# Attention scores of two heads at a time: each head contracted by its own 64 rows of the array, into its own bank, two pairs of heads to a group

## The reference, cut to what matters

```
q, k = rotary_xpos(l2norm(q) * qs, l2norm(k) * ksc)      # 8 heads of 64 channels
sim  = einsum('bhwid,bhwjd->bhwij', q * 8, look_around(k))  # 128 queries x 256 keys
attn = softmax(where(mask, -max, sim))
out  = einsum('bhwij,bhwjd->bhwid', attn, look_around(v))
x    = x + out @ wo
```

## Time and profile before

| | us |
|---|---|
| median of 3 executions | 1212.52 |
| lowest, highest | 1208.71, 1213.76 |
| span of the profiled execution | 1215.7 |
| PE busy in it | 1095.3 |
| DVE, ACT, POOL busy in it | 760.1, 545.0, 364.5 |
| score matmuls (L1719) busy in it | 118.0 |

### The profile page before, as it was taken

The page is one execution under the profiler, slowest core; times in us unless marked ns, Lnnn a source line. Parts: engine busy times, 40 slices in busy tenths (PEclk is TensorE's granted clock), DMA queues, the critical chain, the costliest instruction groups (busy, mean ns, idle before and its releaser), DMA issues.

```text
span 1215.7 us, 18344 instructions
## 1 busy us (share of the span) xinstructions
PE 1095.3 (90%) x5768; PEld 891.3 (73%) x5768; DVE 760.1 (63%) x1886; ACT 545.0 (45%) x1188; POOL 364.5 (30%) x364
## 2 busy tenths in 40 slices
PE   5899799999998898999987699989999898889987
PEld 3677667767686787878876477778878787768776
DVE  7778873666558676667665244666667666644463
ACT  4667423030313565555555233435565555543332
POOL 5212421122124553444440000154435444300020
PEclk9899899999999899999999799999999999999989
DMA  8001020000000000000001000000000000000011
GB/s 303 1 1 52 18 91 1 1 0 0 1 1 19 1 2 18 0 18 0 18 10 53 26 9 9 4 15 2 1 18 0 18 0 26 3 9 9 9 35 35
DMA packets 14330, 25.35 MB, mean 21 GB/s; under 512 B 848, under 2 KB 11208, under 8 KB 13512
## 3 DMA queue, kind: packets, MB, share of 16 engines
q1 hardware_dynamic: 14280, 24.72, 6.2%
HBM read 20.53 MB, written 2.10 MB: 19 GB/s over the span
## 4 chain that ended last, share of the span: by engine, by line
PE 62%; DVE 16%; issue 7%; ACT 6%; DMA 6%; POOL 2%; DVEq 0%; SPq 0%; POOLq 0%; ACTq 0%
PE bank L1433 21%; PE bank L1746 7%; PE bank L1719 7%; DMA shifted<-inner 5%; PE bank L1764 5%; PE bank L1625 5%; PE bank L1577 4%; PE bank L1731 4%; PE bank L1845 3%; DVE conv L585 2%; ACT probs_t L1322 2%; ACT probs L1311 1%; PE bank L1588 1%; DVE scores L897 1%; PE bank L1757 1%
## 5 line engine op out<-in xcount | busy, mean ns | idle before, releaser
L1311 ACT ACTIVATE probs<-scores,row_bias,q_rnorm 128x256 f32<-128x256 f32 (+1 forms) x256 | 144.5, 566 | 161.8 <-DVE row_bias L902 160.8
L1746 PEld LDWEIGHTS bank<-v_tok,probs_t 128*128 128x128 f32 x896 | 114.7, 193 | 50.5 <-ACT probs_t L1322 28.0
L1746 PE MATMUL bank<-v_tok,probs_t 128*128 128x64 f32 x896 | 120.9, 275 | 33.5 <-ACT probs_t L1322 18.6
L1719 PE MATMUL bank<-k_t,q_heads 128*128 128x256 f32 (+1 forms) x512 | 118.0, 364 | 8.4 <-DVE q_heads L886 6.8
L897 DVE CUSTOM_DVE_ANT_0 scores<-bank,mask 128x256 f32<-128x256 f32 (+1 forms) x256 | 89.3, 385 | 26.5 <-PE bank L1719 23.1
L1719 PEld LDWEIGHTS bank<-k_t,q_heads 128*128 128x128 f32 x512 | 87.0, 194 | 17.7 <-issue 8.0
L470 POOL TENSOR_TENSOR norms<-norms,minus_half 128x16 f32<-128x16 f32 x32 | 93.6, 2924 | 2.7
L1433 PE MATMUL bank<-wqkv_hi,x_hi 128*128 128x512 f32 x192 | 89.6, 467 | 1.4 <-ACT v_tok L1288 0.8
L1433 PE MATMUL bank<-t_hi,wm_hi 128*128 128x512 f32 (+1 forms) x192 | 78.2, 407 | 14.1 <-DVE hidden L1055 12.5
L1433 PE MATMUL bank<-wqkv_lo,x_hi 128*128 128x512 f32 x192 | 78.8, 410 | 0.0
L1731 PE MATMUL bank<-ident,probs 128*128 128x128 f32 x448 | 72.8, 280 | 6.2 <-ACT probs L1311 6.2
(11 more groups left out here) (220 smaller groups left out, 2698.2 us busy)
## 6 DMA issues: line engine op xcount, KB each, us to landing
w_stage<-in_wm_l_dram SPq DMA_DIRECT2D x8, 534.0 KB, 3.6
w_stage<-in_wqkv_dram SPq DMA_DIRECT2D x2, 1536.0 KB, 8.0
out_dram<-stream SPq DMA_DIRECT2D x4, 512.0 KB, 2.9
shifted<-inner SPq DMA_DIRECT2D x8, 254.0 KB
stream<-in_x_dram SPq DMA_DIRECT2D x1, 1536.0 KB, 13.2
emb<-in_ctx_dram SPq DMA_DIRECT2D x1, 1536.0 KB, 6.6
inner<-in_w_gate_dram SPq DMA_DIRECT2D x1, 1152.0 KB, 9.3
ew<-in_pos_bias_dram SPq DMA_DIRECT2D x1, 1024.0 KB, 9.8
```

The lines of the kernel that those rows point to most:

```text
L1311: act.activation(probs[:, i % 2, e, 0:nk], scores[:, i % 2, e, 0:nk], ACT.Exp, bias=row_bias[:, w % 2, h:h + 1], scale=q_rnorm[:, w, h:h + 1],
L1719: ins = pe.matmul(bank[6 + i % 2][:, e * 2 * P:e * 2 * P + nk], q_heads[:, 2 * i + e, :], k_t[:, i, k0:(w + 1) * P], start=True, stop=True)
L1746: ins = pe.matmul(bank[3][:, h * DH:(h + 1) * DH], probs_t[:, i % 2, 2 * e + k, :], v_tok[:, w - nk + 1 + k, h * DH:(h + 1) * DH], start=( ...
```

## The change

`q_t` holds the four transposed blocks of q as they are, two heads to a block, without zeros. ACT copies all of it (`queries`); `q_odd` of DVE and the zeroing by POOL are gone. The scores of two pairs are made together: `score_pairs(n, w, 0)` for pairs 0 and 1 stands where `score` 0 and 1 stood, and `score_pairs(n, w, 1)` for pairs 2 and 3 where `score` 2 stood; nothing is left where `score` 3 stood. Each product contracts 64 rows, 0 to 63 for the even head and 64 to 127 for the odd one; even heads go to bank 6 and odd ones to bank 7. `c_qk` counts groups, so `masked` of either pair waits for the whole group, and a group waits until all four masks of the group before it are done.

```diff
-            def q_odd(n):
-                dve.wait_ge(c_t, 2 * n + 2)
-                dve.tensor_copy(q_heads[64:128, :, :]...[:, 1, :, :], bank[2][64:128, :]...).then_inc(c_qo, 1)
...
             def masked(n, w, i, first=False):
-                wait_alone(dve, c_qk, u + 1)
+                wait_alone(dve, c_qk, 2 * n + i // 2 + 1)
                 for e in range(2):
-                    ... bank[6 + i % 2][:, e * 2 * P:e * 2 * P + nk],
+                    ... bank[6 + e][:, (i % 2) * 2 * P:(i % 2) * 2 * P + nk],
...
-            def q_even(n):
+            def queries(n):
                 act.wait_ge(c_t, 2 * n + 2)
-                act.activation(q_heads[0:64, :, :]...[:, 0, :, :], bank[2][0:64, :]..., ACT.Copy).then_inc(c_qe, 1)
+                act.activation(q_t[:, :, :], bank[2][:, :].rearrange("p (c t) -> p c t", t=P), ACT.Copy)\
+                    .then_inc(c_qt, 1)
...
-            def score(n, w, i):
-                u = 4 * n + i
-                if i == 0:
-                    pe.wait_ge(c_qe, n + 1)
-                    pe.wait_ge(c_qo, n + 1)
-                if not (isinstance(u, int) and u < 2):
-                    pe.wait_ge(c_tt, 2 * u - 2)
+            def score_pairs(n, w, g):
+                if g == 0:
+                    pe.wait_ge(c_qt, n + 1)
+                if not (isinstance(n, int) and n == 0 and g == 0):
+                    pe.wait_ge(c_tt, 8 * n + 4 * g)
                 k0 = max(w - 1, 0) * P
-                for e in range(2):
-                    nk = (w + 1) * P - k0
-                    ins = pe.matmul(bank[6 + i % 2][:, e * 2 * P:e * 2 * P + nk], q_heads[:, 2 * i + e, :],
-                                    k_t[:, i, k0:(w + 1) * P], start=True, stop=True)
+                nk = (w + 1) * P - k0
+                for i in (2 * g, 2 * g + 1):
+                    for e in range(2):
+                        half = slice(e * DH, (e + 1) * DH)
+                        ins = pe.matmul(bank[6 + e][:, (i % 2) * 2 * P:(i % 2) * 2 * P + nk], q_t[half, i, :],
+                                        k_t[half, i, k0:(w + 1) * P], start=True, stop=True)
                 ins.then_inc(c_qk, 1)
...
                     transpose_probs(n, w, 0)
-                    score(n, w, 2)
+                    score_pairs(n, w, 1)
...
                         project_o(n - 1)
                         free = [(c_res, n)]
-                    score(n, w, 3)
                     weigh_values(n, w, 1)
...
                     if one:
-                        score(n + 1, (w + 1) % TT, 0)
-                        score(n + 1, (w + 1) % TT, 1)
+                        score_pairs(n + 1, (w + 1) % TT, 0)
                     transpose_o(n, free)
```

More of the change, by code:

```diff
@@ L169, in build @@
         rope_l = sb("rope_l", [P, 4, TT, DH])
-        q_heads = sb("q_heads", [P, HEADS, P])
+        q_t = sb("q_t", [P, KI, P])
         squares = sb("squares", [P, 2, INNER])
@@ L220, in build @@
         (c_zero, c_tab, c_xs, c_xt, c_xt_out, c_p, c_sq, c_v, c_ss, c_clip, c_rn, c_rq, c_rope, c_add,
-         c_kn, c_t, c_kt, c_qe, c_qo, c_qk, c_tt, c_nb, c_ex, c_pt, c_pt_out, c_pv, c_ri, c_on, c_ot, c_ot_out,
+         c_kn, c_t, c_kt, c_qt, c_qk, c_tt, c_nb, c_ex, c_pt, c_pt_out, c_pv, c_ri, c_on, c_ot, c_ot_out,
          c_wo, c_res) = signals(
             "c_zero c_tab c_xs c_xt c_xt_out c_p c_sq c_v c_ss c_clip c_rn c_rq c_rope c_add c_kn c_t "
-            "c_kt c_qe c_qo c_qk c_tt c_nb c_ex c_pt c_pt_out c_pv c_ri c_on c_ot c_ot_out c_wo c_res")
+            "c_kt c_qt c_qk c_tt c_nb c_ex c_pt c_pt_out c_pv c_ri c_on c_ot c_ot_out c_wo c_res")
         (d_shift, d_stats, d_aggr, d_eps, d_rstd, d_norm, d_tp, d_tp_out, d_w1, d_gelu, d_act, d_w2, d_res0) = signals(
@@ L234, in build @@
         w_raw = inner[:, :, :].rearrange("p n d -> p (n d)")
-        C_ZERO = 3
+        C_ZERO = 2
         tiles = lambda b: bass.ts(b, TT) if not isinstance(b, int) else slice(b * TT, (b + 1) * TT)
@@ L510, in _ @@
             copy_tile(1, 1, 1, 1)
-            pool.memset(q_heads[:, :, :], 0.0).then_inc(c_zero, 1)
             rotate(0, 0)
@@ L522, in _ @@
             pool.memset(last_hi[32:64, :].bitcast(F32), 1.0).then_inc(c_zero, 1)
+            pool.wait_ge(c_zero, 3)
+            pool.memset(last_lo[32:64, :].bitcast(F32), 0.0).then_inc(c_zero, 1)
             pool.wait_ge(c_zero, 4)
-            pool.memset(last_lo[32:64, :].bitcast(F32), 0.0).then_inc(c_zero, 1)
-            pool.wait_ge(c_zero, 5)
             pool.memset(shifted[0:1, 0, :], 0.0).then_inc(c_zero, 1)
-            wait_alone(pool, c_zero, 6)
+            wait_alone(pool, c_zero, 5)
             for l in range(LAYERS):
@@ L894, in masked @@
                     dve.wait_ge(c_ex, 2 * u - 2)
-                wait_alone(dve, c_qk, u + 1)
+                wait_alone(dve, c_qk, 2 * n + i // 2 + 1)
                 for e in range(2):
-                    dve.tensor_tensor_reduce(scores[:, i % 2, e, 0:nk], bank[6 + i % 2][:, e * 2 * P:e * 2 * P + nk],
+                    dve.tensor_tensor_reduce(scores[:, i % 2, e, 0:nk],
+                                             bank[6 + e][:, (i % 2) * 2 * P:(i % 2) * 2 * P + nk],
                                              mask[:, 2 * P - nk:2 * P], 1.0, NEG, ALU.add, ALU.max,
@@ L956, in attention @@
                         sum_squares(n + 2)
-                    if one:
-                        q_odd(n + 1)
                     normalise(n, w)
@@ L1038, in ahead @@
                 else:
-                    q_odd(n0)
                     x_low(n0 + 2, 2, bank[1][:, 0:D])
@@ L1351, in attention @@
                     if one:
-                        q_even(n + 1)
+                        queries(n + 1)
                     else:
@@ L1392, in ahead @@
                     keys(n0, 0)
-                    q_even(n0)
+                    queries(n0)
                     x_transposed(n0 + 2, 2, bank[1][:, 0:D])
@@ L1795, in attention @@
                         transpose_q(n + 1, (w + 1) % 2)
-                        free = [(c_qe, n + 2), (c_qo, n + 2)]
+                        free = [(c_qt, n + 2)]
                     else:
@@ L1899, in _ @@
                     pe.wait_ge(b_res, NB * (l + 1))
-                score(n0, 0, 0)
-                score(n0, 0, 1)
+                score_pairs(n0, 0, 0)
                 with pe.Fori(0, NB - 1) as b:
```

4 lines of the change are left out of this document (removed).

## The result

The changed kernel takes 1222.57 us (median of 4 runs, 1217.32 to 1223.13) against 1213.14 (median of 4, 1208.71 to 1214.83) for the kernel before on the same chip: ratio 1.007, 95% interval 1.0043 to 1.0097. It is slower by 9 us. The forecast was 1218.5, with slower the likeliest outcome. The time lies in the range, but the loss did not come from the steady tiles, where I had put it.

The account below looks back on a forecast made before the run. PE was taken as dense, with no slack in the chain scores, mask, exponential, transpose. Six sequences at +1.1 (6.6), about 0.4 per layer's last, less 1.4 at layer starts: +6 us, median 1218.5, range 1200 to 1247.

Parts of the forecast that it names:

- Slots: Each group of eight score products takes five slots of 0.216 us, as starts keep program order; bounds four and eight.
- Price of the change of rows: Switching between 128 and 64 rows at each score group costs 0.10 us going in and 0.19 going out.
- Term 1: First score group, w = 1 to 3: masked 0 and transpose_probs 0 0.32 us later; PE idles some 0.7.
- Term 2: Second score group: project_o 0.83 us later, masked 3 0.40 later; tiles w = 1, 2, 3 longer by 0.30, 0.25, 0.40.
- Term 3: Tile w = 0: group up to 0.45 us later, 0.30 won on the wait for queries; net +0.15.
- Term 4: q_odd leaves DVE, 22.2 us busy: gives 0 at w = 1 to 3, 0.7 credited at each layer start.
- The last sequences: Last sequence of each layer, where no qkv follows: about 0.4 us longer each, masked 3 gaining what PE loses.
- Full pairs, switch hidden: Rival: score groups take four slots with no switch price; w = 1 to 3 tiles 0.43 shorter, 1198.5 us; chance 0.20.
- One at a time: Rival: the row halves don't run side by side in score groups; 37 us longer in all, 1249; chance 0.18.
- The clock: Rival: the new gap ahead of transpose_probs 0 lowers the clock in 24 tiles, costing 29 us, 1247; chance 0.07.

Follow-up runs that it names:

- the one with the same rows: Changed kernel with the odd heads also contracted by rows 0 to 63, so their own scores are left out: 1269.2 us (one run).
- the pair with one product at a time: Two kernels with the new grouping: padded 128-row queries of the kernel before, 1256.55 us; changed kernel with all heads on rows 0 to 63, 1269.2 us.

## Why the prediction was right in time and wrong in its working

**Slots.** I took five, and it is four. This is the step that failed first: "only the second of one head can run beside the first of the next". All eight run in pairs, in either order of the program.

**Price of the change of rows.** I charged 0.10 in and 0.19 out, 0.29 at each group. At the first group 1.07 stands for four slots and the 0.09 that was seen before (1.82 less 0.86 is 0.96), so the price is 0.11. At the second, transpose_probs 0 to group is 0.58 for 0.49, and from the group to the second product of qkv it is 1.40 for 1.09, so 0.40. These are the rows of before, behind the 570.41 of the earlier trace rows:

```profile
570.90 1.03 PE L1719 MATMUL bank<-k_t,q_heads 128*128 128x256 f32 x4
...
571.99 0.39 PE L1433 MATMUL bank<-wqkv_lo,x_hi 128*128 128x512 f32 x1
```

The sum of the two, 0.51, is about the 0.58 that I took; the fifth slot is what made a longer tile of it on paper.

**Term 1,** masked 0 and transpose_probs 0 later by 0.32: 0.01. The idle time of TensorE ahead of it, 0.66 for 0.7, is as forecast by luck: I added 0.45 of time won and 0.32 of delay, and it is 0.75 of time won and no delay. That the chain behind the scores has no slack was read rightly, since a TensorE that is free earlier starts transpose_probs 0 no earlier.

**Term 2,** project_o 0.83 later and masked 3 0.40 later: project_o is 0.40 later, masked 3 is 0.13 earlier. Tiles of w = 1, 2, 3 were to gain 0.25 to 0.40 in length; they lost 0.05 to 0.14. At w = 3 the wait at weigh 2 did grow, from 1.02 to 1.36, since TensorE is there sooner.

**Term 3,** w = 0 up by 0.15: it went from 18.49 to 18.12, both with a fall of the clock; at 1.00 it is 17.38 in the kernel before and 16.68 in the changed one, so the change gains 0.7 there. The wait for the queries is halved as forecast, 0.37 for 0.77:

```profile
539.92 1.08 PE L1737 MATMUL bank<-v_tok,probs_t 128*128 128x64 f32 x4 [1.91 <-ACT probs_t L1316]
...
546.65 0.70 PE L1710 MATMUL bank<-k_t,q_t 64*128 64x256 f32 x4 [0.37 <-ACT q_t L1290]
```

**Term 4,** VectorE 22 us less busy: 26.

**The last sequences,** 0.4 up in each layer: 2.9 over the tiles of w = 1 and 2, and 0.8 more at w = 3 in layer 0. This is the largest miss. I wrote that masked 3 gains there what TensorE loses, and didn't ask what a clock at half does to project_o, behind which masked 3 stands.

**Rivals.** "Full pairs, switch hidden" had the mechanism on TensorE, at 0.20, but left out that the second group still costs 0.40 more than score 2 did, and so promised 0.43 a tile for 0.1. "One at a time" was priced at 1249; the kernel that does just that, the one with the same rows, took 1269.2 (one run). "The clock", at 0.07, holds the loss, but at other places: I looked for it ahead of transpose_probs 0 in the steady tiles, which keep 1.00 in both kernels in the rows shown, and it is at w = 0 and in the last sequences, which had long waits already. "Against it: w = 3 has a gap of 1.02 and keeps 1.00" holds of w = 3 only. No case joined two of them, full pairs and the clock, and that is what happened.

The forecast of +6 for +9.4 is thus luck. Two errors offset each other: +1.1 a sequence that didn't come, and 2.9 a layer where I had 0.4. All but 0.07 of the chance of slower, 0.44, came from cases that were wrong.

## What to carry to other kernels

Shortening the work of an engine that others feed can make it wait, unless its queue is put in a new order at the same time: here the change gave 9 us away as it stood, and with two lines moved (the group ahead of the wait, the mask ahead of the residual) it is 27 us faster than the kernel before (1185.76 against the 1212.86 beside it). After such a change, look first at what is queued behind a wait on every engine, and at the last iterations, where the filling work is missing. And count the granted clock with the waits: new idle time on TensorE can cost more than its own length, and a few spare products in it are a cheap test of whether it does.

## What the runs showed of the hardware

- Two fp32 matmuls of 64 rows each, one in the upper and one in the lower half of TensorE's rows, start 7 ns apart and give two for the time of one, 0.216 at 256 columns. They do it also when the two of one half stand ahead of those of the other in the program (13 to 14 ns apart). The Trainium skill, "TensorE: Matmul & The Clock Gate", Part 2 (Step-by-step: what each phase is for), says that matmuls stay in program order and only weight loads are pulled ahead. The trace of the kernel with the halves in turn doesn't agree in its starts: there eight instructions of the program stand lower, lower, lower, lower, upper, upper, upper, upper, and two of one half can't start 14 ns apart, since in the kernel with the same rows they are 216 ns apart.
- A change from 128 to 64 rows and back cost 0.1 us at the first group of eight and 0.4 at the second, both in the changed kernel and in the pair with one product at a time (0.10 and 0.39).
- The granted clock fell to half (1.2 GHz) behind waits of TensorE of 1.91 us at w = 0 and 2.35 in the last sequence, and stayed at full behind one of 1.36 at w = 3. The length of a wait alone does not settle it: with the mask first, the last sequence of layer 0 kept 1.00 behind a wait of 2.05, and in layer 1 the same tile, behind one of 2.03, was at 0.80. With the spare products at w = 0 alone, that tile of layer 0 kept the full clock behind a wait of 2.45 (its group took 1.13) and fell behind the next, of 2.24 (weigh 2 took 1.97 for 1.11). With the waits filled it stayed at full over the stretches of both attentions that are cut out above. What exactly brings a fall stays open.
- Spare work on a waiting TensorE made the changed kernel 24 us faster (1222.57 to 1198.59).
